# A two-layer transformer block on one core: four batches in flight, biases by the matrix engine, and work moved from VectorE to ScalarE

## The reference, cut to what matters

```python
# LN(t) = (t - mean) / sqrt(var + eps)
# 1. chunked attention with a selective scan
xr = rmsnorm(LN(x)) * norm_w
dt = softplus(xr @ dtl.T @ dt_w.T + dt_b);  B, C = xr @ ...
h[t] = exp(dt[t] * A) * h[t-1] + dt[t] * xr[t] * B[t]       # 16 states
mx = silu(sum_n h * C + xr * D_p);  v = silu(xr @ v_w.T + v_b)
z, r = silu(mx @ ... + b);  u = sigmoid(mx @ ... + bu)
att = softmax(q(z) @ k(z).T + bias) @ v
h = silu(mx @ ... + (att * r) @ h_w.T + bhx + h_b)
x = x + LN(res + u * (h - res))
# 2. gated feed-forward with integer weights: down(silu(gate(LN(x))) * up(LN(x)))
# 3. causal attention, 16 heads of 8, scores = q @ mix @ k.T
# 4. two layers of: local attention (8 heads of 64, window 64, l2-normed and
#    rotated q and k), then y + (a * gelu(g)) @ w2 + b2 after a layer norm (lg, lb)
out = x + LN(y)
```

## Time and profile before

| | us |
|---|---|
| median of 3 runs | 1905.69 (1900.63 to 1914.58) |
| the profiled execution: its own time | 1899.97 |
| its span, first to last instruction | 1898.2 |
| PE busy | 1530.9 (81%), 11540 instructions |
| VectorE busy | 1478.0 (78%), 2885 |
| ScalarE busy | 1082.9 (57%), 2536 |
| GpSimd busy | 381.4 (20%), 279 |
| chain that ended last | PE 43%, DVE 35%, ACT 13%, issue 4%, DMA 3% |

### The profile page before, as it was taken

One profiled execution on the slowest core, in us unless ns is written; L12 is line 12 of the kernel. 1 busy time (PEld: TensorE's weight loads), 2 busy tenths in 40 slices (PEclk: granted clock), 3 DMA queues, 4 the chain that ended last, 5 costly groups with the idle time before them and its releaser, 6 DMA issues.

```text
span 1898.2 us, 30428 instructions
## 1 busy us (share of the span) xinstructions
PE 1530.9 (81%) x11540; PEld 843.3 (44%) x11540; DVE 1478.0 (78%) x2885; ACT 1082.9 (57%) x2536; POOL 381.4 (20%) x279
## 2 busy tenths in 40 slices
PE   3656688889987898877778898888857888999896
PEld 1113433544544555533344455435423453465574
DVE  6999875865489978598998858898699767566855
ACT  4325515437676677635664476377642663687783
POOL 0000000303025234100321214123002112143640
PEclk7678878879999999979899899799978897999999
DMA  6651304200023200415124002232053012000110
GB/s 246 232 169 43 68 3 101 55 4 16 7 66 86 79 9 21 91 59 157 54 100 93 8 13 65 59 107 71 12 163 92 9 49 37 7 21 18 27 24 17
DMA packets 70769, 121.39 MB, mean 64 GB/s; under 512 B 6784, under 2 KB 27904, under 8 KB 68864
## 3 DMA queue, kind: packets, MB, share of 16 engines
q1 hardware_dynamic: 70624, 119.45, 22.5%
HBM read 89.14 MB, written 15.60 MB: 55 GB/s over the span
## 4 chain that ended last, share of the span: by engine, by line
PE 43%; DVE 35%; ACT 13%; issue 4%; DMA 3%; SPq 1%; POOL 1%; DVEq 0%; ACTq 0%
ACT tiles L1688 6%; DVE tiles L1130 6%; PE psum L591 5%; DVE neg_max L1284 5%; PE psum L805 4%; DVE tiles L1124 3%; DVE tiles L1134 3%; PE psum L787 2%; DVE tiles L1057 2%; PE psum L791 2%; DMA tiles<-in_ones 2%; DVE lmax L1365 2%; PE psum L764 2%; PE psum L931 2%; PE psum L940 2%
## 5 line engine op out<-in xcount | busy, mean ns | idle before, releaser
L591 PE MATMUL psum<-cst,tiles 128*128 128x128 f32 x1408 | 223.3, 296 | 111.7 <-DVE tiles L1057 72.7
L591 PEld LDWEIGHTS psum<-cst,tiles 128*128 128x128 f32 x1408 | 170.4, 151 | 192.5 <-DVE tiles L1057 69.2
L1688 ACT ACTIVATE tiles<-psum,lmax,invn 128x128 f32<-128x128 f32 x512 | 226.2, 467 | 40.4 <-DVE lmax L1370 34.5
L639 PE MATMUL psum<-tiles,cst 128*128 128x512 f32 x256 | 155.9, 741 | 65.9 <-DVE tiles L1134 65.8
L1284 DVE TENSOR_REDUCE neg_max<-psum 128x2 f32<-128x768 f32 (+3 forms) x176 | 188.2, 1120 | 21.4 <-PE psum L768 21.1
L1781 POOL TENSOR_TENSOR tiles<-tiles,lsum 128x1024 f32<-128x1024 f32 x64 | 132.3, 2068 | 291.5 <-DVE lsum L1374 291.5
L1770 POOL TENSOR_TENSOR tiles<-tiles 128x512 f32<-128x512 f32 x64 | 85.0, 1329 | 516.6 <-DVE tiles L1335 516.6
L1130 DVE TENSOR_TENSOR_SCAN tiles<-tiles 128x512 f32<-128x512 f32 x128 | 162.0, 1293 | 3.0
L1538 ACT ACTIVATE tiles<-tiles,colp 128x512 f32<-128x512 f32 x128 | 89.2, 723 | 101.7 <-DVE tiles L1130 90.7
L1622 ACT ACTIVATE tiles<-psum 128x768 f32<-128x768 f32 (+1 forms) x128 | 109.8, 922 | 39.7 <-PE psum L791 27.8
L1333 DVE TENSOR_TENSOR tiles<-psum,tables 128x512 f32<-128x512 f32 x128 | 87.5, 684 | 52.7 <-ACT tiles L1638 27.8
(11 more groups left out here) (226 smaller groups left out, 3461.0 us busy)
## 6 DMA issues: line engine op xcount, KB each, us to landing
tiles<-bc_scratch SPq DMA_DIRECT2D x128, 512.0 KB, 4.9
v_prev<-tiles SPq DMA_DIRECT2D x112, 128.0 KB, 2.4
split_scratch<-tiles SPq DMA_DIRECT2D x96, 128.0 KB, 2.4
tiles<-split_scratch SPq DMA_DIRECT2D x32, 384.0 KB
wts<-in_wts SPq DMA_DIRECT2D x1, 3114.0 KB, 15.5
tiles<-in_x SPq DMA_DIRECT2D x8, 256.0 KB, 3.0
out<-tiles SPq DMA_DIRECT2D x8, 256.0 KB, 2.6
tiles<-in_tab SPq DMA_DIRECT2D x1, 768.0 KB, 6.9
```

Of the source, the lines that this page charges most:

```text
L591: ins = nc.tensor.transpose(ps[:, j * 128:(j + 1) * 128], src[:, j * 128:(j + 1) * 128], ident)
L639: ins = mm(place("y_sum", m), ident, T(S6_H[m % 3] + a), start=(m == a == 0), stop=(m == STATES // 2 - 1 and a == 1))
L1688: ins = fn(pr[:, i * 128:(i + 1) * 128], ps[:, i * 128:(i + 1) * 128], ACT.Exp, bias=own(lmax)[:, b, i:i + 1], scale=own(invn)[:, j, 0, 2 ...
```

## The change

Seven edits go together, and the order strings and banks are written anew for them.

1. `STREAMS` goes from 3 to 4 and `TILES` from 21 to 18. To fit, tiles are reused sooner: three decay tiles instead of four, a ring of two token blocks of k instead of four, one `o_cols` tile instead of two, and the squares of q and k share tiles with the rotated halves.
2. Biases that vary along the free dimension (`v_b`, `bu`, `h_b`, `bv`, `bo`, `b2`) are added by TensorE: `biased` puts one product of three bf16 rows (the bias split in three parts) into the bank before the others accumulate. The product with `D_p` becomes one more term of `y_sum`, with a diagonal matrix `skip`. `lg` and `lb` of the last layer norm are folded into `w1` and `b1` in the preparation, and the mean is subtracted by a product with a centring matrix.
3. x*sigmoid(x) is one ScalarE function (`Silu`) straight from PSUM, and u's sigmoid is a tanh of the same table set.
4. The last step of all eight norms goes to ScalarE (`ln_apply`), with a small VectorE instruction `ln_shift` ahead of it. Norms 3 and 5 read PSUM directly.
5. `v_ext`, `o_cols` and `lpT_b` become ScalarE copies.
6. q and k of a token block go together: `lqk_in`, one `qk_sq`, `qk_turned` (one 1024-wide and two 512-wide instructions), one `qk_sum` on POOL.
7. The fetches are in another order (`cst` after five others), with one more of 288 columns; the tables of the norm folding and `bias_split` and two small transfers `bias_rows` are added to the preparation.

Counted in the new strings, ScalarE has 113 table loads instead of 86. Batches are loaded in the order 1, 0, 2, 3, 5, 4, 7, 6.

```diff
-STREAMS = 3
-TILES = 21
+STREAMS = 4
+TILES = 18
...
+DBU, HC, QK_COLS, V_EXT, O_COLS, SHIFT_B, LPT_B = "DVE", "DVE", "DVE", "ACT", "ACT", "DVE", "ACT"
+LN_ON_SCALAR = (0, 1, 2, 3, 4, 5, 6, 7,)
+FETCHES = ("cst", "colp", "wts_s6", "bcst", "rowp", "wts_chunk", "tab", "pre", "ints", "wts_heads", "wts_window")
...
+                def biased(ps, name, i=0):
+                    prepared("fetched", "bcst")
+                    pe.wait_ge(sem("bias_rows"), 32)
+                    a = ROWS[name][0] + i * 128
+                    mm(blocks(ps), bconst("ones", rows=PARTS), bias_parts[:, a:a + 128].unsqueeze(1).to_broadcast([PARTS, NJ, 128]),
+                       start=True, stop=True, skip_group_check=True)
...
                     if m == 0:
-                        take("y_sum", 0, freed_by=[at("yd")])
+                        prepared("skip")
+                        take("y_sum", 0, freed_by=[at("mx")])
+                        mm(place("y_sum", 0), skip[:, :], T(XRT), start=True, stop=False)
...
-                def lq_in(l, j):
-                def lk_in(l, j):
+                def lqk_in(l, j):
                     lhs, a = shifted(l, j)
+                    ps = take("lqk_in", l, j, freed_by=[at("qk_sq", l, j), at("qk_turned", l, j)], banks=2)
+                    mm(ps[:, 0:512], lhs, wts[:, a:a + 512], start=True, stop=True)
+                    full(mm(ps[:, 512:1024], lhs, wts[:, a + 512:a + 1024], start=True, stop=True))
...
                 def l_scores(l, j):
...
-                            earlier = 64 if j > 0 else 0
+                            earlier = 64 if j % 2 else 0
+                            if j == 2:
+                                mm(ps[0:64, o:o + 64], q[r, g, 0:64], k[r, g, before_t:before_t + 64], start=False, stop=True, skip_group_check=True)
...
-                def normed(k, dst, signal, scale=None):
+                def ln_shift(k):
+                    dve.wait_ge(*at("ln_rstd", k))
+                    stt(out=own(shift)[:, k, :], in0=own(mv)[:, k, :, 0], scalar=-1.0, in1=own(rstd)[:, k, :], op0=ALU.mult,
+                        op1=ALU.mult).then_inc(sem("ln_shift"), 1)
...
+                def qk_turned(l, j):
+                    prepared("tables")
+                    if (l, j) > (0, 0):
+                        dve.wait_ge(*product("lq_turn", *back(l, j, 1)))
+                        dve.wait_ge(*product("lk_turn", *back(l, j, 1)))
+                    ps = ready2("lqk_in", l, j)
+                    dve.wait_ge(*at("sum_sq", l, j))
...
+                    tt(t1, v, cos, ALU.mult)
+                    tt(t2[:, :, :, 0:32], v[:, :, :, 32:64], sin[:, :, :, 0:32], ALU.mult)
+                    tt(t2[:, :, :, 32:64], v[:, :, :, 0:32], sin[:, :, :, 32:64], ALU.mult).then_inc(sem("qk_turned"), 1)
...
+                def ln_apply(k):
+                    act.wait_ge(*at("ln_shift", k))
+                    for j in range(NJ):
+                        ins = fn(T(LN_TO[k])[:, j * 128:(j + 1) * 128], ln_in(k)[:, j * 128:(j + 1) * 128], ACT.Identity,
+                                 bias=own(shift)[:, k, j:j + 1], scale=own(rstd)[:, k, j:j + 1])
...
+                def sp_exp():
+                    step(fn(T(SPE), ps, ACT.Abs, bias=col("dt_b")))
+                    fn(T(SPZ), ps, ACT.Relu, bias=col("dt_b"))
...
+                def mx():
+                    table(SILU)
+                    act.wait_ge(*product("y_sum", STATES // 2 - 1))
+                    fn(T(MX), psum[:, bank[batch[0], "y_sum", (0,)], :], ACT.Silu).then_inc(sem("mx"), 1)
...
+                def qk_sum(l, j):
+                    pool.wait_ge(*at("qk_turned", l, j))
+                    tt(T(TURNED, 2), T(TURNED, 2), T(TURNED + 2, 2), ALU.add).then_inc(sem("qk_sum"), 1)
```

More of the change, by code:

```diff
@@ L59 @@
 NROWS = _n
+NBIAS = ROWS["qs"][0]
 WTS = {}
@@ L71 @@
 _n = 0
-for _name, _w in (("ident", 128), ("mean", 128), ("causal", 128), ("blocks", 128), ("taps", 32),
-                  ("eps", 1)):
+for _name, _w in (("ident", 128), ("mean", 128), ("centre", 128), ("eps", 1)):
     CST[_name] = (_n, _n + _w)
@@ L182, in banks_of @@
 def banks_of(name):
[L184 removed]
+    return 2 if name in ("scores", "probs_turn", "row_scores", "pair_scores", "lqk_in", "l_scores") else 1
 def begins(name, args):
@@ L603, in bias_products, with shift_products @@
                     full(mm(ps[:, 128:384], staged[:, 128:256], staged[:, 256:512], start=True, stop=True))
+                def shift_products():
+                    prepared("fetched", "colp")
+                    prepared("fetched", "wts_window")
+                    ps = take("shift_products", freed_by=[once("hidden_bias")])
+                    for i in range(2 * DEPTH * HIDDEN_CHUNKS):
+                        t, l, c = i // (DEPTH * HIDDEN_CHUNKS), i // HIDDEN_CHUNKS % DEPTH, i % HIDDEN_CHUNKS
+                        m = HID_ROWS[c]
+                        ins = mm(ps[0:m, i:i + 1], wt("w1", l * 2 * HID + t * HID + c * 128, m), col("lb", l), start=True, stop=True)
+                    full(ins)
                 def xr_turn():
@@ L911, in f_mean @@
                     pe.wait_ge(*at("shift2_b", l))
-                    full(mm(take("f_mean", l, freed_by=[at("centred", l)]), const("mean"), T(HT2), start=True, stop=True))
+                    full(mm(take("f_centre", l, freed_by=[at("centred_sq", l), at("f_norm", l)]), const("centre"), T(HT2), start=True, stop=True))
                 def f_var(l):
@@ L1426, in _ @@
-                run("DVE", {"decay": decay, "qk_scale": qk_scale, "h_bias": h_bias, "bias_operands": bias_operands, "score_bias": score_bias_rows,
-                            "mix": head_mix, "ffw": ffw_values, "tables": rotary_tables, "ln_stats": ln_stats, "mean_sq": mean_sq, "res": res,
-                            "xr": xr, "sp_z": sp_z, "v_raw": v_raw, "sp_1pe": sp_1pe, "sp_rest": sp_rest,
-                            "dt_sum": dt_sum, "dtu": dtu, "dbu": dbu, "h": h, "hc": hc, "yd": yd, "mx": mx, "v_rows": v_rows, "z": z,
-                            "q_cols": q_cols, "k_cols": k_cols, "r": r, "u_raw": u_raw, "score_max": score_max, "probs": probs, "hr": hr,
-                            "h_raw": h_raw, "gated": gated, "ln_apply": ln_apply, "x_new": x_new, "fxn": fxn, "fg": fg, "fh": fh, "fo": fo,
-                            "axn": axn, "k_res": k_res, "k_split": k_split, "q_res": q_res, "q_split": q_split, "v_ext": v_ext,
-                            "row_max": row_max, "max_parts": max_parts, "o_cols": o_cols, "ao_part": ao_part, "aout": aout, "y_norm": y_norm,
-                            "shift_b": shift_b, "q_turned": q_turned, "k_turned": k_turned, "sum_sq": sum_sq, "l_bias": l_bias, "l_inv": l_inv,
-                            "lpT_b": lpT_b, "y1": y1, "shift2_b": shift2_b, "centred": centred, "f_norm": f_norm, "hgb": hgb, "hh": hh,
-                            "y_raw": y_raw, "y_next": y_next, "out": out})
@@ L1741, in _, with bias_split, step @@
                 tt = nc.gpsimd.tensor_tensor
+                steps = [0]
+                def bias_split():
+                    pool.wait_ge(*fetched("rowp"))
+                    rows, rest = staged_rows[0:1, 0:NBIAS], staged_rest[:, 0:NBIAS]
+                    first, (second, third) = bias_parts[0:1, :], staged_parts
+                    h_b, bhx = (rows[:, ROWS[n][0]:ROWS[n][1]] for n in ("h_b", "bhx"))
+                    def step(ins):
+                        steps[0] += 1
+                        ins.then_inc(sem("pool_step"), 1)
+                        pool.wait_ge(sem("pool_step"), steps[0])
+                    step(tt(h_b, h_b, bhx, ALU.add))
+                    step(nc.gpsimd.tensor_copy(first, rows))
+                    step(tt(rest, rows, first, ALU.subtract))
+                    step(nc.gpsimd.tensor_copy(second, rest))
+                    tt(third, rest, second, ALU.subtract).then_inc(sem("bias_split"), 1)
                 def v_zero():
```

915 lines of the change are left out of this document (422 added, 493 removed).

## The result

The changed kernel takes 1777.27 us (median of 4 runs, 1774.65 to 1784.77) against 1904.81 for the kernel before (4 runs, 1900.63 to 1914.58). The ratio is 0.9319, 95% interval 0.9287 to 0.9351. The profiled execution took 1777.72 us with a span of 1775.9.

A forecast was written before the change was run, and what follows sets the result against it. VectorE was taken to be late most often, with PE's own work the floor. Start 208, middle 1531 (1393 us of PE work at 91%), tail 48 and launch/end 2 sum to 1789, predicted as 1790 us; range 1690 to 1880.

The forecast's parts named there:

- The middle: Stretch between start and tail, 200 to 1850 us before; forecast 1393 us of PE work at 91%, 1531 us.
- the 35 that I added: PE's new bias, skip and score products in the middle: 35 of 41 us, bounds 0 and 41.
- half of the 51: PE's clock in the middle rising from 0.91 to 0.944 gives back 25 us, between 0 and 51.
- The 91%: PE's busy share of the middle after the change, with ends 84% and 95%.
- thirteen slices: 50 us slices before with VectorE busy under 38 us and PE 90%, taken as the state after the change.
- sign of being wrong at the root: PE's busy share outside start and tail staying at 84% with VectorE at 67%.
- only open waits elsewhere: Rival: fourth batch brings nothing, PE stays at 84% in the middle; 1916 us, chance 0.04.
- the 8 that I took: Start: first norm waits for `cst`, fetched after five others; 8 us, between 0 and 14.
- the 208: Start, the scan of the first batches: 200 us plus 8 for the later fetch of `cst`.
- ScalarE late: Rival: ScalarE becomes the late engine, PE's 67 us of waits on it in the middle double; 1857 us, chance 0.16.
- Longer q and k chain: Rival: q and k some 3.2 us later in 64 blocks, 205 us latency, holds PE; 1940 us, chance 0.08.
- Fuller PE: Rival: PE reaches 95% in the middle and its clock gives the whole 51 us; 1697 us, chance 0.22.

The follow-up runs named there:

- three-batch runs: Kernel before, its three batches and order kept: VectorE's instructions made short, then ScalarE and TensorE loaded too; 1883.53 us and 1937.55 us.
- the light VectorE: Kernel before, three batches and old order, VectorE's instructions made short in place, output not the reference's; 1883.53 us, ratio 0.9885.
- the new loads: Kernel before, three batches, short VectorE instructions, plus extra ScalarE copies and doubled TensorE turns to approach the changed kernel's loads; 1937.55 us, ratio 1.017.

## Why the prediction was right, and where its reasons were not

**The sum.** Forecast 208 + 1531 + 48 + 2 = 1789; the trace has 200 + 1530 + 46 + 2. The middle was hit by two errors that cancel. PE's work in it was forecast at 1418 before the clock and 1393 after it; it was 1375: the clock went to 0.94 as forecast, but it gave back some 43 us, not 25, if the new work came to the 35 that I added. I had taken half of the 51 because weight loads need not shrink; nearly the whole came back. And PE's share was 89.9%, not 91%. That 1531 met 1530 is luck.

**VectorE's relief, the failed reason.** The 91% was read from thirteen slices of the trace before in which VectorE was little busy, and the text said that these are the state after the change. The three-batch runs show that this was a coincidence of numbers. Taking 120 us off VectorE brought 22 us, and PE stayed at 80% wherever VectorE was busy. PE's share of the middle was 84% before, 85% with the light VectorE, 85% with the new loads and 90% in the changed kernel. My own sign of being wrong at the root, a share that stays at 84% with a lighter VectorE, is what the light kernel shows (VectorE 71% of its middle). The forecast came out because the change brought more than the relief on which it was built. The rival that the 280 us "only open waits elsewhere" (1916 us, chance 0.04) came nearest to what happens without the fourth batch: 1884 with the relief alone, 1938 with nearly all the loads. What the text gave half a sentence and no number, that "a fourth batch offers PE other work when one chain is late", stands, with the order and the shorter chains, for 97 us or more of the 128 by the estimate above. Slices in which one engine is busy and the other not differ in much beside that load; they are no experiment.

**The loads.** VectorE: forecast -280 to 1198, measured -221 to 1257. The turning came out as forecast (1219 + 682 + 681 ns, 2.58 us per token block), `ln_shift` at 276 ns for 250. Summed over the rows of all groups VectorE's instructions fell by 251 us, from 1575.5 to 1324.5; 29 are missing. The sum lacked a term for instructions that become slower beside GpSimd (L1240 alone grew by 14), and with both wide GpSimd instructions in halves the rows fell by another 28, to 1296.3. The rest is overlap: neighbouring instructions overlap in the records, busy time counts the overlap once, and a sum of row times, as I used it, does not. ScalarE: forecast +192 to 1275, measured +172 to 1255. The terms came out: `ln_apply` 102.8 us busy for 101, 113 loads at 1283 ns, the copies 62.7 for 64. The first of them is luck again: an `ln_apply` takes 482 or 457 ns where I had said about 0.4 us would confirm it, 122 us by count and mean, and the overlap of neighbours brings that down to 102.8. All of ScalarE's rows together rose by 200 us, from 1260.8 to 1460.8, and its busy time by 172: the difference is overlap again. As before, ScalarE was idle for only 2.7 us ahead of all its table loads. TensorE: bias products 21.5 us for 17, `skip` 8.7 for 10.

**Start and tail.** The first norm waited 1.3 us for `cst`, against the 8 that I took (it had waited 3.7 before, so the other order of the fetches cost nothing there). The 200 of the start is my cut and no measurement of the 208: PE did 1.8 us less work in it than before. The tail was 46 for 48.

**The rivals.** *ScalarE late*: its waits rose to 88.9 us where I had said near 70, and 133 would have been the rival. It is the larger of the two now, and its price per us of load rose to 0.41, so the rival had the direction. The rule of the Trainium skill (ScalarE: Activation LUTs, Rules for kernel authors) that was weighed there did not hold for this edit: undoing it costs 15 us. *Longer q and k chain*: its terms give 7.2 - 4.35 = 2.85 us a block, 182 us over all, and not the 3.2 and 205 that I used; that changes no chance. PE's waits on GpSimd are 0.8 us of the middle, so next to nothing of it was exposed; the sum took 2434 ns where I had put 2.07 us, and did its harm by another way, through VectorE. *Fuller PE*: not reached; the clock gave back 43 of its 51 us, but the share stayed at 90%, not 95.

## What to carry to other kernels

Before crediting a gain to an engine's lighter load, take the load off and change nothing else: here a 120 us lighter VectorE was worth 22 us, though 76 us more cost 46. Where engines take turns at being late and each is 70 to 85% busy, another independent batch in flight, with an order that uses it, may be worth more than any move of work between them. To see which, follow the largest waits for steps that a change leaves alone: if they stay when the loads move and go with the new order, the order did it. Fusing two instructions on GpSimd saved 13 us of its own time here and cost 19 on VectorE, some of whose instructions out of SBUF end only with GpSimd's.

## What was unexpected of the hardware

- A VectorE instruction of 8 columns that normally takes 0.17 us took up to 1.89 us, and one of 0.69 us took 2.87, each beside a GpSimd instruction that had begun before; 21 of 64 such 8-column products ended within 0.03 us of GpSimd's end. With the sum of q and k in halves the mean of the first fell from 470 to 292 ns, and with both wide ones in halves to 259.
- The same 11,540 instructions kept TensorE busy for 1531 us in the kernel before and 1546 in the light one, at a granted clock of 0.895 and 0.884 in the two profiled executions (medians over the runs of one chip 0.894 and 0.8885). The changed kernel has 0.93. What made the light kernel's clock lower is not shown.
- Cutting a VectorE instruction down to 8 columns leaves much of its time: the copy out of PSUM took 155 ns (679 with 512 columns), the statistics 153 (279 with 128).
